# Graph attention and relational messages on one core: a fused edge loop whose ScalarE work goes by pairs of steps

## The reference, cut to what matters

```python
h = jnp.maximum(_layernorm(x, axis=-1), 0.0)
Q = (h @ Wq).reshape(n, H, HD); K = (h @ Wk).reshape(n, H, HD); V = (h @ Wv).reshape(n, H, HD)
score = jnp.einsum('ehd,ehd->eh', Q[dst], K[src]) / np.sqrt(HD)
score = score + jax.nn.relu(efeat @ W1 + b1) @ W2 + b2        # the edge network
m = jax.ops.segment_max(score, dst, num_segments=n)
ex = jnp.exp(score - m[dst])
alpha = ex / jax.ops.segment_sum(ex, dst, num_segments=n)[dst]
x = x + jax.ops.segment_sum(alpha[:, :, None] * V[src], dst, num_segments=n).reshape(n, D) @ Wo + bo
# then layer 1: x + relu(segment_sum(message(rel, src) * norm * gate, dst))
```

## Time and profile before

| | us |
|---|---|
| median of 3 runs | 5446.73 (5445.96 to 5447.83) |
| the profiled execution | 5449.73 |
| its span | 5447.9 |

### The profile page before, as it was taken

How to read it: one execution, slowest core, us unless ns; L and a number is a source line. 1 busy time by engine, 2 the same in 40 slices (tenths; PEclk the granted TensorE clock), 3 DMA queues, 4 the chain that set the end, 5 groups by cost and what they waited for, 6 DMA issues and landing times. The chain is left out here.

```text
span 5447.9 us, 89819 instructions
## 1 busy us (share of the span) xinstructions
PE 4660.0 (86%) x20748; PEld 2699.6 (50%) x20749; DVE 3301.0 (61%) x7106; ACT 3291.8 (60%) x7926; POOL 3285.8 (60%) x3364
## 2 busy tenths in 40 slices
PE   8799999999999999998899999777777777676766
PEld 5455555555555555555444444344444444444443
DVE  6489999999999999999633333333333333333334
ACT  3489999898999999897544444333333333333333
POOL 0277777777777777777200000477777777777776
PEclk9899999999999999999899999866666666767777
DMA  4588888888888888887434344333333333333334
GB/s 139 161 242 239 238 241 241 238 240 239 240 241 241 242 238 239 236 240 230 146 140 142 139 142 141 124 105 105 105 105 105 105 105 105 105 105 105 105 105 141
DMA packets 542017, 932.63 MB, mean 171 GB/s; under 512 B 102705, under 2 KB 351631, under 8 KB 541712
## 3 DMA queue, kind: packets, MB, share of 16 engines
q0 software_dynamic: 208384, 648.75, 41.3%
q1 hardware_dynamic: 333328, 280.23, 15.9%
HBM read 795.82 MB, written 132.87 MB: 170 GB/s over the span
## 5 line engine op out<-in xcount | busy, mean ns | idle before, releaser
L1033 POOL DMA_INDIRECT kv_rows<-kv_d,idx x1664 | 1695.7, 1019 | 671.4 <-issue 380.7
L1813 PE MATMUL m_sums<-m_rows,m_oh 128*128 x3328 | 1389.5, 566 | 590.3 <-ACT m_rows L1793 517.3
L1750 POOL DMA_INDIRECT m_rows<-msg_d,m_idx x1568 | 1487.4, 949 | 507.2 <-issue 472.7
L1793 ACT ACTIVATE m_rows<-m_rows,m_norm 128x256 f32<-128x256 f32 x1568 | 710.8, 500 | 1267.5 <-DMA m_rows<-msg_d,m_idx 1267.5
L1813 PEld LDWEIGHTS m_sums<-m_rows,m_oh 128*128 128x128 f32 x3328 | 836.1, 275 | 1143.8 <-issue 1021.2
L1835 DVE TENSOR_TENSOR agg<-agg,m_sums 128x256 f32 x832 | 350.2, 421 | 1297.1 <-PE m_sums L1813 1293.7
L1227 PE MATMUL sums<-kv_rows,onehot 128*128 128x264 f32 x3328 | 942.2, 406 | 17.9 <-issue 10.0
L1227 PEld LDWEIGHTS sums<-kv_rows,onehot 128*128 128x128 f32 x3328 | 570.3, 191 | 398.4 <-issue 226.0
L1683 PE MATMUL p_m<-wr,h1T 128*128 128x512 f32 x1568 | 711.1, 597 | 0.0
L1184 PE MATMUL p_q<-shelf,pickT 128*128 x4992 | 696.1, 275 | 12.2 <-ACT pickT L1090 9.5
L1067 ACT ACTIVATE hid<-p_hid,b1s 128x512 f32<-128x512 f32 x784 | 494.3, 682 | 194.2 <-PE p_hid L1164 193.1
(11 more groups left out here) (194 smaller groups left out, 3903.0 us busy)
## 6 DMA issues: line engine op xcount, KB each, us to landing
msg_d<-msg SPq DMA_DIRECT2D x196, 512.0 KB, 2.9
dsts<-dstrow_d SPq DMA_DIRECT2D x208, 256.0 KB
ef_raw<-in_edge_attr_dram SPq DMA_DIRECT2D x195, 256.0 KB
kv_rows<-kv_d,idx POOLq DMA_INDIRECT x1664, 3.9
m_rows<-msg_d,m_idx POOLq DMA_INDIRECT x1568, 2.7
kv_d<-kvo SPq DMA_DIRECT2D x49, 260.0 KB, 2.1
pens<-pens_d SPq DMA_DIRECT2D x52, 192.5 KB
emlp<-mlp_d SPq DMA_DIRECT2D x52, 128.0 KB
```

The source lines that it names most:

```text
L1033: pool.indirect_dma_start(rows[:, lane, k, a:a + KV], None, kv_d[:, :], bass.IndirectOffsetOnAxis(idx[:, half, c:c + 1], 0)).then_inc(gath ...
L1750: pool.indirect_dma_start(rows[:, u, k, :], None, msg_d[:, :], bass.IndirectOffsetOnAxis(idx[:, u // HALF, c:c + 1], 0)).then_inc(gathered ...
L1793: last = nc.scalar.activation(rows[:, u, k, :], rows[:, u, k, :], ACT.Copy, scale=norm[:, bass.ds(2 * g + k, 1)])
L1813: last = nc.tensor.matmul(sums[u % BANKS][:, 0:D], onehot[:, u % HOTS, k, :], rows[:, bass.ds(slot, 1), k, :].rearrange("p a d -> p (a d)" ...
```

## The change

- **ACT by pairs.** `measure` and `pick` become `select_pair(s+2)` in the even steps: one absolute difference and one relu over 512 elements for two steps, the second waiting for the first. `hot` is one relu over 512 elements for two steps, in the odd steps, with the four far_dst of the two steps ahead of it. Buffers grow: far_node by two, far_dst to four, onehot to four.
- **Chunk work over more steps.** On PE `score`, `up`, `down` and `turn_drop` stand in the steps 0, 2, 4 and 5. On DVE the forward scan is in step 0, the backward scan and first_node in step 1, the chain's first part (`carry`) in step 2, its second (`join`) in step 3, `drop` in step 4. `weights` moves to step 5, LATE from R + 3 to R + 5.
- **An edge network piece per step** on PE: `hidden(0)`, `mlp_out(0)`, `hidden(1)`, then `mlp_out(1)` and the next quad's `turn_ef`. On ACT `take_ef` and behind it `take_mlp` stand in the quad's step 0, ahead of `select_pair`; `take_hidden` in the steps 1 and 3, behind the four far_dst and ahead of `hot`.
- **SP** stores the network's output first, loads destinations a quad earlier, has two buffers for edge features, and loads a chunk's tables a quad ahead of the network's output.

The diff, cut:

```diff
-LATE = R + 3
+LATE = R + 5
-HOTS2 = 2
+HOTS2 = 4
@@ SP
             def body(i):
...
-                    if is_step(U * m + U):
-                        load_dsts(m + 1, (v + 1) % 2)
+                    if is_quad(m):
+                        store_mlp(m)
+                    if v % U == U - 1 and is_chunk(c):
+                        load_mlp(c, min(m + 1, CHUNKS))
+                    if is_step(U * (m + 2)):
+                        load_dsts(m + 2, v % 2)
+                    if is_quad(m + 3):
+                        load_ef(m + 3)
                     if v % U == 0 and is_chunk(c + 1):
                         load_idx(c + 1, (v // U + 1) % 2)
-                    if v % U == U - 1 and is_chunk(c):
-                        quads = m + 1 if not isinstance(m, int) else min(m + 1, CHUNKS)
-                        load_chunk(c, quads)
-                    if is_quad(m + 3):
-                        load_ef(m + 3)
-                    if is_quad(m + 1):
-                        store_mlp(m + 1)
+                    if v % U == U - 2 and is_chunk(c):
+                        load_chunk(c)
@@ ACT
+            def select_pair(s):
+                m, u, n = s // U, s % U, s // 2
                 if u == 0:
-                    act.wait_ge(dsts_in[x], 16 * (n + 1))
...
+                    act.wait_ge(dsts_in[m % 2], 16 * (m // 2 + 1))
+                wait(act, pick_ready, n)
+                nc.scalar.activation(far_node[:, :, :], dsts[:, m % 2, u:u + 2, :], ACT.Abs, scale=-1.0,
+                                     bias=t["node"][:, 0:1]).then_inc(far_ready, 1)
+                act.wait_ge(far_ready, n + 1)
+                wait(act, q_done, s + 2 - PICKS)
+                nc.scalar.activation(pickT[:, s % PICKS:s % PICKS + 2, :], far_node[:, :, :], ACT.Relu, scale=-1.0,
                                      bias=t["one"][:, 0:1]).then_inc(pick_ready, 1)
...
+            def hot(s):
+                act.wait_ge(fard_ready, 2 * s + 4)
+                wait(act, summed, s + 2 - HOTS2)
+                nc.scalar.activation(onehot[:, s % HOTS2:s % HOTS2 + 2, :, :].rearrange("p s k n -> p (s k) n"), far_dst[:, :, :],
+                                     ACT.Relu, scale=-1.0, bias=t["one"][:, 0:1]).then_inc(hot_ready, 1)
...
-                    if is_step(s + 3):
-                        measure(s + 3, (u + 3) // U % 2, (u + 3) % U, QUADS // 2 * i + (u + 3) // (2 * U))
-                    if is_step(s - LATE):
+                    if u % 2 == 1 and is_step(s - LATE):
                         measure_dst(s - LATE)
-                    if is_quad(m + 1):
-                        if u % U < 2:
-                            take_hidden(m + 1, u % U)
-                        elif u % U == 2:
-                            take_mlp(m + 1)
-                    if u % U == 3 and is_quad(m + 2):
-                        take_ef(m + 2)
-                    if is_step(s + 3):
-                        pick(s + 3, (u + 3) % PICKS)
-                    if is_step(s - LATE):
-                        hot(s - LATE, (u - LATE) % HOTS2)
-                    if u % R == 3 and is_chunk(c):
+                    if u % U == 0 and is_quad(m + 1):
+                        take_ef(m + 1)
+                    if u % U == 0 and is_quad(m):
+                        take_mlp(m)
+                    if u % U == 1 and is_quad(m + 1):
+                        take_hidden(m + 1, 0)
+                    if u % U == 3 and is_quad(m + 1):
+                        take_hidden(m + 1, 1)
+                    if u % 2 == 0 and is_step(s + 2):
+                        select_pair(s + 2)
+                    if u % 2 == 1 and is_step(s - LATE):
+                        hot(s - LATE)
+                    if u % R == 5 and is_chunk(c):
                         weights(c, (u // R - 1) % 2)
@@ PE
-                    if is_chunk(c) and u % R < 4:
+                    if is_chunk(c):
                         if u % R == 0:
                             score(c, (u // R - 1) % 2)
-                        elif u % R == 1:
+                        elif u % R == 2:
                             up(c)
-                        elif u % R == 2:
+                        elif u % R == 4:
                             down(c)
-                        else:
+                        elif u % R == 5:
                             turn_drop(c)
                     if is_quad(m + 1):
                         if u % U == 0:
                             hidden(m + 1, 0)
                         elif u % U == 1:
                             mlp_out(m + 1, 0)
+                        elif u % U == 2:
                             hidden(m + 1, 1)
-                        elif u % U == 2:
+                        else:
                             mlp_out(m + 1, 1)
-                    if u % U == 2 and is_quad(m + 2):
+                    if u % U == 3 and is_quad(m + 2):
                         turn_ef(m + 2)
@@ DVE
-                    if is_chunk(c) and u % R < 3:
+                    if is_chunk(c):
                         if u % R == 0:
-                            scans(c)
+                            forward(c)
                         elif u % R == 1:
-                            chain(c, R * c)
-                        else:
+                            backward(c, R * c)
+                        elif u % R == 2:
+                            carry(c)
+                        elif u % R == 3:
+                            join(c)
+                        elif u % R == 4:
                             drop(c)
```

## The result

| | median us | runs |
|---|---|---|
| before | 5447.28 | 4 (5445.96 to 5448.83) |
| after | 5471.78 | 4 (5471.18 to 5472.15) |

A forecast was written before the change was run, and what follows sets the result against it. PE bounds the kernel between chunk works; a chunk becomes 26.0 + 2 x (10.62 + 0.47) = 48.2 us against 46.65, +73 over 48 chunks, +75 with the drain, giving 5520 us; range 5400 to 5555.

The forecast's parts named there:

- limit of 1.72 us of waiting: PE alone needs 44.93 us of a 46.65 us chunk, so at most 1.72 is waiting.
- Part 1: ACT's pairs save it 3.3 us in a chunk; as ACT isn't the bound, worth nothing by itself.
- Part 2: ACT's chain from turn_ef to mlp_out(0) holds PE 0.47 us in each of two quads, 0.94 per chunk.
- plain quads: The two quads of a chunk without chunk work, forecast at 10.62 + 0.47 us each.
- Part 3: Chunk work over five steps makes PE lose 2.31 us per chunk, against 1.72 at most before.
- issue gap ahead of score: A gap of 0.35 us on PE ahead of the score, counted in what PE alone needs.
- top ends 7.50: In step 1 DVE's backward scan, taken as 1.26 us long, ends at 7.50 from PE's start of step 0.
- loss of 2.31: PE's summed waits for DVE in the chunk steps, among them 0.39 ahead of up, 0.84 down, 0.83 turn_drop.
- The forecast's own rival: DVE keeps ahead in the chunk steps if busy under 11.6 us: 5366 us (0.14), or 5411 with ACT's loop (0.06).
- Part 4: The rest: SP's loads and POOL's lead cost nothing, two more draining steps cost +2 us.
- only part 3 bites: Rival: ACT never holds PE at mlp_out; chunk 47.2 us, +0.6, time 5477 us; chance 0.14.
- three signs of being wrong: Score distance below 46.6, DVE waiting for PE in steps 1 to 4, ACT's take_ef-to-hid chain under 4.2 us.

The follow-up runs named there:

- e3: The kernel before with only POOL's own weighing moved one step later: 5424.5 us.
- e15: e8 with POOL's weighing one step later: 5461.2 us.
- e1: The kernel after with the four far_dst moved behind take_hidden on ACT: 5426.7 us.
- e5: The kernel after with the pair's absolute difference (far_node) as two activations of 256 instead of one of 512: 5488.6 us.
- e12: e3 with DVE's put one step earlier, in step 14 of the chunk instead of 15: 5425.6 us.
- e4: The kernel before with only SP's new order, earlier destination loads and two buffers for edge features: 5454.4 us.
- e6: e1 with the chunk work spread over eight steps and LATE at R + 7: 5777.5 us.
- e7: The kernel after with POOL's weighing one step later: 5477.1 us.
- e11: e1 with the edge network's pieces on PE back in their old places and take_hidden(1) in step 2 on ACT: 5487.6 us.
- e13: e1 with POOL's weighing one step earlier: 5445.9 us.
- e8: e1 with the chunk work back at the places of the kernel before: 5496.7 us.

## Why the prediction was right in sign and wrong in size

The runs give four steps from before to after that close. Times in medians, chunk lengths beside them:

| step | from, to | us | per chunk |
|---|---|---|---|
| POOL's weighing off the backward scan | before, e3 | -23 | -0.57 |
| new edge order, ACT's pairs (without loop), SP's order | e3, e15 | +37 | +0.69 |
| chunk work over five steps | e15, e1 | -34 | -0.71 |
| far_dst ahead of take_hidden: the loop | e1, after | +45 | +0.96 |
| sum | before, after | +25 | +0.37 |

(e15 carries POOL's weighing a step later than e1 and after have it, and in e1 it meets DVE's weighing, in e15 it doesn't; the second and third rows share what this is worth.)

**What bounds the kernel.** PE between the chunk works, DVE in them: right. e1 and e3 gain 0.6 per chunk against the limit of 1.72 us of waiting that the forecast drew from the earlier trace rows.

**Part 1, ACT's load.** The load fell as forecast: far_node and pickT last 0.715 and 0.722, ACT is busy for 73.8 us less in the thousand (830.9 after, 904.7 before) and waits longer. That this is worth nothing by itself is argued from ACT's waits; no run has the pairs alone. The rule of the Trainium skill that the forecast weighed ("Perfetto Trace Analysis", section "Optimizing Scalar/DVE Operations": smaller instructions, where Scalar isn't saturated but makes others wait) names the right concern, bubbles that ACT makes on PE, but e5 shows a limit of its remedy: cut into smaller ones, the pair's absolute difference made PE wait 0.18 longer, since the reader (pick) needs both. What helped was the order (e1); single steps throughout, in the new order, were not run.

**Part 2, ACT's loop.** Right in mechanism, place and size: forecast 0.94 a chunk, 0.47 in each of two quads; measured 0.48 in each, 43 waits in 21 chunks, and 0.96 when e1 takes it away. (The plain quads themselves grew by 0.54.)

**Part 3, the chunk work.** Wrong, in sign too. Eight steps were to last 26.0 and last 24.70. The terms, from select's start in step 0 (1541.50):

| term | forecast | trace after |
|---|---|---|
| issue gap ahead of score, and select | 0.35, 0.75 | 0, 0.66 |
| add of step 0 starts | 4.52 | 3.99 |
| backward scan and first_node, to the next start | 1.39 | 0.78 |
| carry | 1.28 | 1.09 |
| join | 0.79 | 0.79 |
| drop | 1.71 | 1.70 |
| DVE without a gap | 13.9 | 13.04 |
| PE loses ahead of up | 0.39 | 0 |
| ahead of down (mean of 21: 10.5 / 21) | 0.84 | 0.50 |
| ahead of turn_drop (14.1 / 21) | 0.83 | 0.67 |

The step that failed is "top ends 7.50": it takes the backward scan's 1.26 from the earlier trace rows as the instruction's own duration. It was the duration under a collision, which this very change removes (0.68 after; e3 shows the cause). The forward scan just ahead of it in the timeline of before, as large, should have raised the question:

```profile
1533.03 0.68 DVE L1292 TENSOR_TENSOR_SCAN fwd<-pens,p_soft 128x256 f32<-128x256 bf16 x1
```

The forecast even set the two beside each other ("were it as long as the backward one") and went on. 0.61 of the 0.87 by which DVE was overestimated is this term, 0.19 is carry. The second failed term is the issue gap of 0.35, carried over as if it were PE's own; by e12 it was a wait for DVE. With the shorter score and select it puts the add of step 0 at 3.99 instead of 4.52. So turn_drop starts at 1558.68 - 1541.50 = 17.18 and not at 18.58: 0.53 by the earlier add, 0.87 by DVE's shorter stretch, and this is the 1.30 of the eight steps but for 0.1. What stood against the loss of 2.31 was 1.17 in the rows of waits, and some 0.3 in step 3, where select starts 1.02 behind sums instead of 0.89 and lasts 1.01 instead of 0.82.

The pattern was right: from the add on DVE works without a gap until turn_drop, and PE waits for it ahead of down and turn_drop. The forecast's own rival named 11.6 us as the point from which DVE would stay ahead; the trace lies at 13.04, so that rival didn't come either.

**Part 4.** SP nothing (e4: some +6 on the kernel before), drain +2 (1.7 behind the last score), POOL's lead nothing (it waits 1.2 us for sums in the thousand): right for R + 5. The forecast gave as its reason that the product implies the sums; e6 shows how near that edge was.

**The sum.** 48.2 against 47.02: part 3 is 1.30 too large (26.0 against 24.70), the two plain quads 0.14 too small (11.09 against 11.16 each). Between the first score and the last the forecast had +73 where the trace has +18.4; less the 1.9 us at the start, which it didn't have, that is the 53 us between its 75 and the span's 22. None of the rivals was the case. The one nearest in time, "only part 3 bites" (5477), has both signs of its reasons wrong: part 3 gained and ACT's loop bit. The forecast's own sign held because part 2 outweighs part 3 (+1.08 against -0.71 a chunk); of its two reasons one was right, so there is luck in it. None of the forecast's three signs of being wrong appeared: they didn't ask whether the scan would still last 1.26.

## What to carry to other kernels

Before a duration from a trace goes into a forecast, look at its minimum and median over all instances and at the same shape elsewhere; where they differ, find what ran beside it, since the change may move it. When instructions are fused or moved on an engine that isn't the bound, write out what stands between its two points of contact with the engine that is (here turn_ef to hid), and put what has no input from there (far_dst) behind the second point: the order cost 45 us. Parts of a hand-made order can't be priced one by one: in these runs spread chunk work and spread edge pieces gain only together.

Two kernels beat both: e3, the kernel before with POOL's weighing a step later (5424.5), and e1, the kernel after with the far_dst behind take_hidden (5426.7). They can't be told apart, nor can e12 (5425.6), which is e3 with one step more.

## What the runs showed of the hardware

**A DVE instruction that reads two tensors from SBUF waits for a GpSimd tensor operation beside it.** POOL's weighing (L1039, two operands in SBUF, 1.08 to 1.10 us in 51 of its 52 instances in every trace) beside DVE:

| DVE instruction | operands | alone us | beside POOL's weighing, mean us |
|---|---|---|---|
| backward scan, before | SBUF, SBUF | 0.69 | 1.33 (45 hits) |
| backward scan, e7 | SBUF, SBUF | 0.68 | 1.27 (11) |
| weighing, e1 | SBUF, SBUF | 0.70 | 1.44 (49) |
| weighing, e11 | SBUF, SBUF | 0.70 | 1.50 (51) |
| place, e13 | SBUF, SBUF | 0.34 | 1.54 (31) |
| first_node, e3 | SBUF, one scalar from SBUF | 0.30 | 1.00 (11) |
| forward scan, after | SBUF, PSUM | 0.69 | 0.69 (44) |

The forward scan of the chunk shown above runs at 1543.57 for 0.69 us, wholly inside POOL's 1543.31 to 1544.40, and is not lengthened; the product, the copies from PSUM and the reduction, each with at most one tensor in SBUF, were not either. One tensor in SBUF isn't always enough to be spared: first_node, a comparison with a scalar, is lengthened too. The two don't share the time but stand in line: wherever they begin, the lengthened scans of before end 0.56 behind POOL, the weighings of e1 0.57 to 0.58, the places of e13 0.16.

Once in every trace, in the last chunk, it is POOL that waits. In the kernel before:

```profile
2649.94 0.71 DVE L1354 TENSOR_TENSOR kv_rows<-kv_rows,wgt 128x528 f32<-128x528 f32 x1 [0.84 <-ACT wgt L1115]
2649.99 1.60 POOL L1039 TENSOR_TENSOR kv_rows<-kv_rows,wgt 128x528 f32<-128x528 f32 x1 [16.18 <-ACT wgt L1115]
```

Both had waited for the same weights, DVE began 0.05 ahead and kept its usual 0.71, and POOL took 0.51 longer.

The Trainium skill states this rule: "SBUF — State Buffer", section "Who interferes with whom", has a DVE instruction with two SBUF inputs contend with a GpSimd instruction that reads SBUF, one of them blocked entirely until the other is done. The traces agree on both points. It also says that the one that issues first gets the shared pair of ports. The last chunk agrees with that. Elsewhere DVE lost even where its record starts first (place at 1527.30, POOL at 1527.86); a POOL span is rough, so this stays open.

**"issue" can be a wait.** PE's gap of 0.35 ahead of the score, for which the profile names no other engine, went when DVE's place came a step earlier (e12); in e1 PE waits there once in the thousand, 0.5 us for a load, and the gap came back when place was held up (e13: 7.9 us, 17 times).

**A wait of PE can cost more than its length.** In e8, behind a wait of 1.58 us, the granted clock was 0.55 over the next 3.4 us, and two groups of matmuls took 3.66 us to the next start where they take 2.05 at full clock (1513.74 to 1517.40 against 1505.81 to 1507.87). In the kernel after, whose longest wait of PE in the thousand is 0.7, the clock was 1.00 throughout it.
